# A perceiver layer on one core: sums a slot later, a one-step bias of the exponential, and another order of the stages

## The reference

```
x = x + xattn(layernorm(x), ctx)     # softmax(q k^T / 16) v, added to its own input, times Wo
x = x + mixer(layernorm(x))          # in_w, 3-tap convolution, silu -> u; x_proj -> delta, B
                                     # state = exp(delta*A) * state + delta*u*B   (16 states, 512 channels, 32 steps)
                                     # y = sum of the states + u*D, times out_w
x = x + ffn(layernorm(x))            # silu(gate) * up, down; activations and weights quantised
```

## Time and profile before

| | |
|---|---|
| median of 3 runs | 1031.91 us (1031.9 to 1033.83) |
| profiled execution | 1036.67 us, of which the span from the first to the last instruction is 1034.5 us |
| busy share of the span | TensorE 89%, VectorE 86%, GpSimd 82%, ScalarE 73% |
| scans of blocks 0 to 7 | from 85.3 us to 992.4 us of the span |
| blocks 1 to 6 | 116.4 to 117.5 us each |
| granted clock of TensorE, mean | 0.98 |

### The profile page before, as it was taken

One profiled execution on the slowest core, in us unless ns is written; L12 is line 12 of the kernel. 1 busy time (PEld: TensorE's weight loads), 2 busy tenths in 40 slices (PEclk: granted clock), 3 DMA queues, 4 the chain that ended last, 5 costly groups with the idle time before them and its releaser, 6 DMA issues. The chain is left out here.

```text
span 1034.5 us, 13058 instructions
## 1 busy us (share of the span) xinstructions
PE 925.0 (89%) x4158; PEld 488.3 (47%) x4192; DVE 894.5 (86%) x1216; ACT 756.4 (73%) x1323; POOL 852.8 (82%) x616
## 2 busy tenths in 40 slices
PE   8886988999989999899989999899989999867896
PEld 6642453545435453545435454545435454423454
DVE  1635888899989999899989999899989999899965
ACT  2356657877797859877797859877797869666555
POOL 1059998899979898899979898898979898899920
PEclk9998989999999999999999999999999999989999
DMA  9804710445042610545043610535033400500000
GB/s 354 333 34 163 289 59 2 162 147 202 0 150 99 243 42 2 183 143 205 0 128 115 246 44 2 184 125 223 2 109 120 161 0 2 184 0 0 1 21 21
DMA packets 21915, 116.33 MB, mean 112 GB/s; under 512 B 3479, under 2 KB 4119, under 8 KB 9304
## 3 DMA queue, kind: packets, MB, share of 16 engines
q1 hardware_dynamic: 16232, 80.70, 21.2%
q10 hardware_dynamic: 5616, 34.81, 9.4%
HBM read 111.04 MB, written 4.46 MB: 112 GB/s over the span
## 5 line engine op out<-in xcount | busy, mean ns | idle before, releaser
L1172 DVE TENSOR_TENSOR_SCAN state<-decay,state 128x512 f32<-128x512 f32 (+1 forms) x352 | 590.5, 1696 | 35.3 <-ACT decay L932 22.8
L861 POOL TENSOR_TENSOR state<-w,brep 128x512 f32<-128x512 f32 (+1 forms) x352 | 612.5, 1771 | 0.5 <-POOL w L894 0.4
L1326 PE MATMUL acc<-state,ident 128*128 128x512 f32 x832 | 412.3, 612 | 15.7 <-DVE state L1172 13.8
L932 ACT ACTIVATE decay<-delta,neg_a 128x496 f32<-128x496 f32 x512 | 329.6, 669 | 89.7 <-DVE state L1172 88.6
L1326 PEld LDWEIGHTS acc<-state,ident 128*128 128x128 f32 x832 | 148.5, 193 | 165.5 <-issue 111.9
L869 POOL TENSOR_TENSOR state<-state 128x512 f32<-128x512 f32 x96 | 122.2, 1273 | 45.8 <-DVE state L1172 44.3
L1326 PE MATMUL bank<-xn_t,in_w 128*128 128x512 f32 x128 | 62.0, 618 | 5.0 <-DVE u L1318 3.4
L1326 PE MATMUL bank<-out_w,u 128*128 128x256 f32 x256 | 58.2, 383 | 8.7 <-DVE u L1159 8.7
L916 ACT ACTIVATE soft<-x_in,nmr,rstd 128x256 f32<-128x256 f32 x64 | 33.2, 589 | 42.9 <-POOL nmr L825 42.9
L966 ACT ACTIVATE sg<-bank,ag 128x512 f32<-128x512 f32 x64 | 43.6, 681 | 24.0 <-PE bank L1326 23.1
L894 POOL TENSOR_TENSOR w<-delta,u 128x512 f32<-128x512 f32 x32 | 39.9, 1269 | 22.7 <-ACT delta L1068 22.7
(11 more groups left out here) (170 smaller groups left out, 1318.2 us busy)
## 6 DMA issues: line engine op xcount, KB each, us to landing
keys<-in_keys_t SPq DMA_DIRECT2D x32, 1028.0 KB, 6.0
brep<-b_scratch ACTq DMA_DIRECT2D x32, 1024.0 KB, 6.8
keys<-in_keys_n SPq DMA_DIRECT2D x29, 1024.0 KB
out<-x_in SPq DMA_DIRECT2D x16, 256.0 KB, 5.0
x_in<-in_x SPq DMA_DIRECT2D x14, 256.0 KB
u<-in_keys_n SPq DMA_DIRECT2D x1, 1024.0 KB
w<-in_keys_n SPq DMA_DIRECT2D x1, 1024.0 KB
delta<-in_keys_n SPq DMA_DIRECT2D x1, 1024.0 KB
```

What stands on the lines that cost most here:

```text
L861: nc.gpsimd.tensor_tensor(state[g % CPT][:, 0:count * tok].rearrange("p (c t) -> p c t", c=count), w[:, m, 0:tok].unsqueeze(1).to_broadcas ...
L932: last = nc.scalar.activation(decay[:, q:q + groups * GSEQ, 1:LEN], d, ACT.Exp, scale=neg_a[:, m, n + i:n + i + 1])
L1172: nc.vector.tensor_tensor_scan(flat, by, flat, 0.0, ALU.mult, ALU.add).then_inc(scan_done, 1)
L1326: return nc.tensor.matmul(o, l, r, start=first, stop=last)
```

## The change

Y_AT becomes 1: VectorE takes the sums of tiles 0 to 2 after the scan of the next tile's slot 1. TensorE no longer has sums at slot 0 (FIRST_SUM = 1): it adds the states of slots 0 and 1 together at slot 1, and waits for y there. The part s_neg is gone: the query and key-bias weights are scaled by -1/16 when they are prepared, so that the scores come out negated and scaled, the reduction is a minimum, and one scalar_tensor_tensor makes the bias of the exponential (the tile nmx and its semaphore go with it). The tables SECOND, PRE, PRE_END, POST_FIRST and POST are replaced; FIRST loses s_neg alone; POST_END, LAST, TAIL and PREPARE stay.

```diff
-Y_AT = 0
+Y_AT = 1
...
+FIRST_SUM = 1
+def sum_slot(k):
+    return max(k + 2 if k in PAIRED else k, FIRST_SUM)
-SUMS = [[k for k in range(CPT) if k + 2 * (k in PAIRED) == c] for c in range(CPT)]
+SUMS = [[k for k in range(CPT) if sum_slot(k) == c] for c in range(CPT)]
...
-                                             bias=ebias[:, g:g + 1], scale=SCALE,
+                                             bias=ebias[:, g:g + 1], scale=-1.0,
...
-                nc.vector.tensor_copy(qk_w[:, :, :].rearrange("p h d -> p (h d)"), bank[:, A, :])
-                nc.vector.tensor_copy(q_bias[:, :], acc[:, 0:HALVES])
-                nc.vector.tensor_copy(kb_col[:, :], acc[:, 4:4 + HALVES])
-                nc.vector.tensor_copy(kb_const[:, :], acc[:, 8:9]).then_inc(w_ready, 1)
+                for to, of in (...):
+                    last = nc.vector.tensor_scalar(to, of, -SCALE, None, ALU.mult)
+                last.then_inc(w_ready, 1)
...
-                        nc.vector.tensor_reduce(mx[:, one], bank[:, att_banks(g, scan)[0], 0:KEYS], AX.X, ALU.max)\
+                        nc.vector.tensor_reduce(mx[:, one], bank[:, att_banks(g, scan)[0], 0:KEYS], AX.X, ALU.min)\
                             .then_inc(max_done, 1)
-                    elif part == "s_neg":
+                    elif part == "s_bias":
                         one = slice(g, g + 1)
                         reach(dve, kb_ready, b, 1)
                         reach(dve, max_done, b, g + 1)
-                        nc.vector.tensor_scalar(nmx[:, one], mx[:, one], kb[:, one], -SCALE, ALU.add, ALU.mult)\
-                            .then_inc(nmax_done, 1)
-                    elif part == "s_bias":
-                        one = slice(g, g + 1)
-                        reach(dve, nmax_done, b, g + 1)
-                        nc.vector.tensor_scalar(ebias[:, one], kb[:, one], SCALE, nmx[:, one],
-                                                ALU.mult, ALU.add).then_inc(ebias_ready, 1)
+                        nc.vector.scalar_tensor_tensor(ebias[:, one], mx[:, one], kb[:, one], kb[:, one],
+                                                       ALU.add, ALU.subtract).then_inc(ebias_ready, 1)
...
-                        if c == 0:
+                        if c == SUM_SLOTS[0]:
                             reach(pe, y_ready, b, m)
```

The entries of PRE (pre of blocks 2 to 7) that the prediction speaks of:

```diff
-    ("stats1", [1]),
+    ("stats1", [0]),
-    ("turn1", [3]),
+    ("turn1", [4]),
-    ("q_evac", [10]),
+    ("q_evac", [9]),
-    ("query", [4]),
+    ("query", [5]),
-    ("score", [6, 11, 24, 27]),
+    ("score", [6, 14, 24, 28]),
-    ("s_max", [14, 16, 26, 34]),
+    ("s_max", [14, 17, 25, 35]),
-    ("s_neg", [14, 17, 27, 35]),
-    ("s_bias", [14, 19, 27, 38]),
+    ("s_bias", [15, 22, 27, 38]),
-    ("exp", [13, 20, 28, 38]),
+    ("exp", [15, 22, 28, 37]),
-    ("add1", [45]),
+    ("add1", [17]),
-    ("attn_out", [45, 45]),
+    ("attn_out", [47, 48]),
-    ("x1", [50, 51]),
+    ("x1", [49, 51]),
-    ("u_evac", [58, 59, 64, 64]),
+    ("u_evac", [59, 60, 63, 65]),
-    ("tap0", [60, 61, 65, 65]),
+    ("tap0", [59, 61, 64, 66]),
-    ("silu", [61, 67, 67, 67]),
+    ("silu", [59, 67, 67, 68]),
-    ("dt", [72, 72, 85, 86]),
+    ("dt", [72, 79, 86, 86]),
-    ("softplus", [83, 87]),
+    ("softplus", [81, 87]),
-    ("times_u", [82, 82, 85, 85]),
+    ("times_u", [81, 84, 87, 87]),
```

and of POST (post of blocks 1 to 5; POST_FIRST is the same list for block 0):

```diff
-    ("out_proj", [2, 2]),
+    ("out_proj", [1, 3]),
-    ("x2", [4, 5]),
+    ("x2", [5, 5]),
-    ("hidden", [16, 18, 20, 30, 43, 50, 63, 69]),
+    ("hidden", [16, 18, 24, 30, 43, 48, 64, 69]),
-    ("up", [10, 14, 17, 23, 37, 44, 51, 65]),
+    ("up", [9, 13, 17, 25, 37, 43, 51, 64]),
-    ("finish", [31, 63, 77, 86]),
+    ("finish", [32, 64, 78, 87]),
```

More of the change, by code:

```diff
@@ L121 @@
 SECOND = [
[L122 to L127, removed]
+    ("add1", [37]),
+    ("p_turn", [11, 19, 29, 37]),
+    ("dt", [74, 75, 80, 80]),
+    ("stats1", [0]),
+    ("add2", [70]),
+    ("softplus", [80, 86]),
+    ("q_evac", [9]),
+    ("attn_out", [45, 45]),
+    ("exp", [11, 15, 24, 33]),
+    ("s_max", [11, 15, 19, 31]),
+    ("z_evac", [15, 30, 36, 43]),
+    ("turn2", [55]),
@@ L128 @@
     ("rstd2", [51]),
+    ("s_bias", [12, 16, 21, 33]),
+    ("x1", [49, 50]),
+    ("score", [10, 11, 16, 23]),
+    ("u_evac", [60, 64, 70, 70]),
     ("tap0", [63, 63, 69, 70]),
[L130 to L145, removed]
-    ("x1", [50, 51]),
-    ("tap2", [64, 66, 69, 70]),
-    ("stats1", [0]),
-    ("s_neg", [15, 19, 23, 32]),
+    ("turn1", [5]),
     ("times_u", [82, 83, 87, 87]),
-    ("q_evac", [12]),
-    ("p_last", [17, 21, 26, 36]),
+    ("query", [7]),
+    ("p_last", [12, 17, 24, 35]),
+    ("x_dbl", [75]),
+    ("attend", [12, 25, 33, 39]),
     ("rstd1", [0]),
-    ("query", [5]),
@@ L155 @@
-    ("mix_in", [58, 60, 65, 68]),
-    ("attn_out", [46, 46]),
+    ("mix_in", [58, 61, 66, 70]),
+    ("evac1", [4]),
+    ("p_evac", [14, 24, 31, 39]),
+    ("x_proj", [72]),
+    ("zt_evac", [17, 30, 37, 43]),
+    ("p_sum", [13, 19, 28, 37]),
+    ("silu", [65, 66, 70, 70]),
+    ("b_load", [79, 84, 84, 87]),
+    ("tap2", [63, 64, 69, 70]),
+    ("stats2", [50]),
+    ("xn1", [1]),
+    ("z_turn", [13, 27, 35, 44]),
+    ("evac2", [55]),
     ("xn2", [53]),
-    ("s_bias", [15, 20, 23, 34]),
@@ L214 @@
[L214 to L245, removed]
+    ("rstd1", [0]),
+    ("dt", [72, 79, 86, 86]),
+    ("q_evac", [9]),
+    ("tap0", [59, 61, 64, 66]),
@@ new lines @@
+    ("turn2", [54]),
+    ("zt_evac", [24, 31, 36, 46]),
+    ("p_evac", [20, 27, 32, 40]),
+    ("stats1", [0]),
+    ("s_bias", [15, 22, 27, 38]),
+    ("z_evac", [21, 30, 34, 43]),
+    ("evac2", [56]),
+    ("stats2", [52]),
+    ("u_evac", [59, 60, 63, 65]),
+    ("xn2", [53]),
+    ("rstd2", [51]),
+    ("s_max", [14, 17, 25, 35]),
+    ("score", [6, 14, 24, 28]),
+    ("turn1", [4]),
+    ("times_u", [81, 84, 87, 87]),
+    ("tap2", [59, 62, 66, 66]),
+    ("x_proj", [69]),
+    ("add2", [65]),
@@ L246 @@
+    ("softplus", [81, 87]),
+    ("add1", [17]),
+    ("z_turn", [23, 28, 33, 44]),
+    ("xn1", [4]),
+    ("mix_in", [57, 58, 61, 62]),
+    ("attend", [20, 27, 32, 42]),
+    ("p_turn", [17, 26, 31, 39]),
+    ("x1", [49, 51]),
+    ("p_sum", [22, 26, 31, 40]),
+    ("attn_out", [47, 48]),
+    ("exp", [15, 22, 28, 37]),
+    ("p_last", [17, 23, 28, 37]),
+    ("b_load", [77, 78, 83, 86]),
+    ("x_dbl", [72]),
+    ("silu", [59, 67, 67, 68]),
+    ("evac1", [5]),
+    ("query", [5]),
 ]
 POST_FIRST = [
-    ("h_evac", [32, 35, 73, 79]),
@@ L267 @@
[L267 to L270 removed]
+    ("gate", [15, 18, 20, 28, 39, 46, 58, 69]),
+    ("out_proj", [1, 3]),
+    ("h_floor", [22, 32, 57, 74]),
+    ("finish", [32, 64, 78, 87]),
+    ("xn3", [9]),
+    ("x_max", [10]),
+    ("tanh", [14, 18, 20, 27, 39, 46, 57, 68]),
+    ("x_evac", [13]),
+    ("h_max", [20, 31, 54, 71]),
+    ("scale_h", [27, 34, 70, 75]),
+    ("down", [32, 60, 73, 80]),
+    ("y_last", [0]),
@@ L279 @@
[L279 to L284, removed]
-    ("x_turn", [7]),
[L286 to L294, removed]
+    ("gate", [15, 18, 20, 28, 39, 46, 58, 69]),
@@ new lines @@
+    ("out_proj", [1, 3]),
+    ("h_floor", [22, 32, 57, 74]),
+    ("finish", [32, 64, 78, 87]),
+    ("xn3", [9]),
+    ("x_max", [10]),
+    ("tanh", [14, 18, 20, 27, 39, 46, 57, 68]),
+    ("x_evac", [13]),
+    ("h_max", [20, 31, 54, 71]),
+    ("scale_h", [27, 34, 70, 75]),
+    ("down", [32, 60, 73, 80]),
+    ("y_last", [0]),
+    ("x_turn", [7]),
+    ("h_evac", [32, 35, 72, 80]),
+    ("hidden", [16, 18, 24, 30, 43, 48, 64, 69]),
+    ("x2", [5, 5]),
+    ("scale_x", [11]),
+    ("h_scale", [25, 32, 59, 74]),
```

90 lines of the change are left out of this document (37 added, 53 removed).

## The result

| | before | after |
|---|---|---|
| median | 1032.96 us (6 runs, 1031.9 to 1034.09) | 1090.07 us (6 runs, 1077.22 to 1108.87) |
| ratio, 95% interval | 1 | 1.0508 [1.0452, 1.0565] |
| profiled execution | 1036.67 us, span 1034.5 | 1093.79 us, span 1092.0 |
| VectorE busy | 894.5 us, 1216 instructions | 933.3 us, 1184 instructions |

What follows compares the result with a forecast made beforehand. VectorE paces most slots, but TensorE, almost gapless up to attn_out, holds x1. Six steady blocks at -0.15 (-0.9) and -0.2 in the first block's attention give -1.1: profiled 1036.67 to 1035.6, median 1030.8 us; range 1024.5 to 1036.

Steps and rivals of the forecast that it cites:

- the price of the new instruction: On VectorE, the one-column scalar_tensor_tensor that makes the exponential's bias was taken as equal to the old s_bias, 0.21 us.
- Steady block: Blocks 1 to 6: -0.35 up to x1 and +0.2 after it, net -0.15 us each from 116.5.
- y of tile 1: VectorE's sum step at slot 22: its wait of 0.72 us goes, since scan 1 (1.2 us) gives more cover.
- x1's second half: VectorE's step after attn_out on TensorE: comes at 66.4 us instead of 66.7, with a wait before it of over 0.5.
- scan 42: Near the block's end: waits 2.1 us for its decay because softplus moved earlier, instead of scan 43 waiting 1.2.
- Finish of group 0: VectorE's step ahead of x1: arrives at 44.8 us, TensorE's down ends about 45.3, a new wait of 0.5.
- TensorE's start of the block: Without slot 0's sums, TensorE idles 0.8 us before turn1; scores begin at 15.6 us against 15.4.
- What is taken from VectorE alone ahead of x1 is paid back at x1.: TensorE runs almost without a gap from query to attn_out, where x1 starts; of 0.72 + 0.7 us saved, 0.35 is left.
- One-step bias: Four instructions leave VectorE per block, two of 0.25 us and two of 0.10: 0.7 us less.
- Late sums: Sums a slot later: VectorE loses a 0.72 us wait; TensorE pays nothing for tiles 1 to 3, only at the block's start.
- Rival 2: Clock halves about 19 us into each steady block at TensorE's thin stretch: five more blocks pay 1.0 us, 1036; chance 0.22.
- Rival 3: ScalarE drains about 1.38 us at each table load, so moved softplus costs 0.5 us in six blocks: 1034; chance 0.03.

Runs made afterwards that it cites:

- the kernel with the mended bias: The changed kernel with the bias of the exponential made by tensor_scalar with two per-partition scalar columns instead of scalar_tensor_tensor; 1040.32 us, ratio 1.0065.
- the query first: The kernel with the mended bias, with the query moved from step 5 to 4, ahead of the merged sums of slots 0 and 1; 1034.12 us, ratio 0.9997.
- 2.3 us less of TensorE's work per block: The query first plus early sums in the last block (1031.01 us), without bias instruction, key-bias evacuation and 16 one-column matmuls; 1032.03 us, ratio 0.9981.
- the run with tensor_tensor: The query first plus early sums in the last block (1031.01 us), with the bias replaced by tensor_tensor of the row minimum with itself; 1080.42 us, ratio 1.044.
- the two SBUF tensors in the kernel before: The kernel before with only the bias's second step rewritten as scalar_tensor_tensor, kb and nmx both in SBUF; 1081.37 us, ratio 1.0436.
- softplus later: The query first, with softplus of tiles 0 and 1 two steps later, behind the decays of slot 42; 1046.66 us, ratio 1.0111.

## Why the prediction was wrong

The step that failed is the price of the new instruction: "The new scalar_tensor_tensor on one column isn't in the trace; between the row's s_bias (0.21) and nothing more, I take it as equal." It measured 51.6 us for 32, 1.61 each in the mean and 6.93 at most. Its upper bound was taken from an instruction with another kind of operands. No row of before showed a VectorE instruction in the scans with two tensors in SBUF, and that should have been the reason for a wide bound and a rival. The row was there for the bound, too: GpSimd is busy 105.0 of 116.5 us, so a VectorE instruction that must wait for it will nearly always have to. None of the three rivals had this mechanism; they all kept VectorE's busy time as it was.

The other points, read in the kernel with the mended bias, where they can be seen:

- **Steady block.** Predicted 116.35 (116.5 - 0.15); a block without a fall of the clock takes 116.4, and 116.3 with the query first. The accounting of the lists held.
- **y of tile 1.** Its wait is gone, as predicted. **x1's second half** waits 0.73 ("with a wait before it of over 0.5"), **scan 42** waits 2.10 ("scan 42 waits 2.1"), **y_last** 0.84 (under 1.5), **tap0** 0.48 (predicted 0.55), **scan 31** 0.27 (0.35).
- **Finish of group 0** was to wait 0.5 for down; it waits 0.2 at most. The list was late by some 0.3 there.
- **TensorE's start of the block.** Idle before turn1 0.73 against 0.8 predicted. The scores were put at 15.6 and begin at 15.9 (555.96 - 540.03). The prediction's zero, 543.0, is the end of y_last; with stats1 moved ahead of scan 0, that point now lies 1.7 before the first scan (540.03 and 541.76 here). Counted from it, x1's second half begins at 66.5 in a block without a fall, against 66.4 predicted.
- **"What is taken from VectorE alone ahead of x1 is paid back at x1."** The wait at x1 is there, but the reason that TensorE is behind doesn't hold: with 2.3 us less of TensorE's work per block, most of it ahead of x1, the wait stays at 0.73, and the 0.2 us by which VectorE is early at scan 22 is still there behind x1. What sets the wait is closer: in that run TensorE begins the sum of slot 19 when scan 19 ends (51.02 and 50.96 into the block), and from there to the end of attn_out (64.3) it has no gap.
- **One-step bias.** The saving on VectorE's side was put at 0.7 us of its time per block, of which, together with the 0.72 of the sums, 0.35 was to be left at x1; alone, in the old order, it is 0.3 per block (116.2 against 116.5).
- **Late sums.** "For tiles 1 to 3 that costs nothing" is borne out with the new order, where the steady block comes out as predicted; with the old one the same edit costs 27 us. The prediction priced the parts one by one, and such a price holds for one order of the stages only.
- **Rival 2**, the clock near 19 us at 1.0 us each. It was the right mechanism for what is left: four blocks of eight with a fall near 16 us, at 0.9 to 1.1 in the two of them that can be compared (117.3 and 117.5 against 116.4), and one with a fall near 72 us, at 1.7. It gave 1036; measured were 1040.3. The last block's loss (2.8 us, from the late sums) was in no term: "Blocks 7 and after keep their tables: 0" overlooked that the sums' slots hold for the last block as well.
- **Rival 3**, the drain at each load of a table, isn't supported: scan 42 waits what the list without it gives, 2.10.

## What to carry to other kernels

Before an instruction is exchanged for a "shorter" one, compare where its operands lie, not only its engine and size: on VectorE, beside a busy GpSimd, a second tensor in SBUF turned 0.2 us into as much as 8.03; a per-partition scalar or an operand in PSUM avoids it. Where busy time rises while instructions fall in number, look at the least and the longest duration of each group before looking at waits. An order of stages and the slot of a dependency are one design: tested apart here they cost 6% and 2.5%, and together, with one step moved, nothing that can be measured.

## What was not expected of the hardware

- A waiting VectorE instruction isn't always served at the next boundary between GpSimd's instructions. At 601.23 in after it came while GpSimd was in its second of five, and the three behind it all went first. At the same place of two blocks of one execution (the run with tensor_tensor) the instruction took 8.03 and 0.99 us. In the traces of after, of the two SBUF tensors in the kernel before and of tensor_tensor, 68 of the 96 took over 0.25 us. Of these, 56 ended at the first end of a GpSimd instruction; the other 12 were passed over until GpSimd had nothing ready, and it then stood idle for 3.4 to 10.6 us. None was served at a boundary in between. The rule of the Trainium skill ("SBUF — State Buffer", SBUF: two separate sides), that whoever starts first holds the ports for the whole instruction, doesn't tell of this. What decides between the two outcomes is open; it is probably also why runs of such kernels scatter over 1% to 3% (1073.82 to 1084.83; 1073.3 to 1090.49; 1077.22 to 1108.87).
- The scan, with one of its tensors in PSUM, doesn't feel GpSimd: in the trace of after a scan of two states takes 2.28 us in the mean both beside a GpSimd that is busy throughout (111 of them) and beside an idle one (22).
- The granted clock answers to shifts of under a microsecond. The kernels with the query first, with softplus later and with the one-column matmuls left out do the same work or less, and have two, eight and two falls in blocks 1 to 6 of their one profiled execution each; their times are 1034, 1047 and 1032 (the last has the early sums in its last block too, which are worth 3 us).
